# A mixture-of-experts kernel on one Trainium2 core: two pieces of row preparation change places on VectorE and on GpSimd

## What is computed

```python
def cond(hidden, ids):                      # adapter and layer norm, chosen per batch
    z = relu(hidden @ down_w[id] + down_b[id])
    y = hidden + z @ up_w[id] + up_b[id]
    return layernorm(y) * ln_g[id] + ln_b[id]
def ffn(h):                                 # h: 16 x 256 rows of 256
    p = softmax(h @ gate_w + gate_b)        # 8 experts, the two best, weights normalised
    out = h + mlp(h, shared weights)
    return out + sum over the two best e of weight_e * mlp(h, weights of expert e)
x = x + ffn(cond(x, itok))                  # mlp: 256 -> 1024, gelu, 1024 -> 256
```

## Time and profile before

| | |
|---|---|
| median of three runs | 622.54 us (621.13 to 623.94) |
| the profiled execution, its own time | 623.3 us |
| its span, from the first to the last instruction | 621.6 us |
| granted TensorE clock, mean | 0.993 |
| TensorE busy | 596.2 us, 96% |
| VectorE busy | 498.0 us, 80% |
| GpSimd busy | 404.6 us, 65% |
| ScalarE busy | 386.1 us, 62% |

### The profile page before, as it was taken

The page is one execution under the profiler, slowest core; times in us unless marked ns, Lnnn a source line. Parts: engine busy times, 40 slices in busy tenths (PEclk is TensorE's granted clock), DMA queues, the critical chain, the costliest instruction groups (busy, mean ns, idle before and its releaser), DMA issues.

```text
span 621.6 us, 16955 instructions
## 1 busy us (share of the span) xinstructions
PE 596.2 (96%) x5119; PEld 484.7 (78%) x5119; DVE 498.0 (80%) x1218; ACT 386.1 (62%) x666; POOL 404.6 (65%) x326
## 2 busy tenths in 40 slices
PE   7889999999999999999999999999999999999993
PEld 3556576677666678888878888888888999899882
DVE  3999878977867866998989898989897677888862
ACT  1776956776867747766676767676754455455450
POOL 3453868887646612559678686858697566666682
PEclk8999999999999999999999999999999999999998
DMA  8999679694675954676556766666634454243322
GB/s 282 291 221 244 175 177 290 146 271 110 155 120 182 289 135 149 145 124 143 122 128 105 147 129 140 129 139 128 94 50 71 62 67 61 54 67 64 45 25 28
DMA packets 119046, 85.52 MB, mean 138 GB/s; under 512 B 71346, under 2 KB 106418, under 8 KB 118962
## 3 DMA queue, kind: packets, MB, share of 16 engines
q1 hardware_dynamic: 100802, 60.64, 40.0%
q0 software_dynamic: 15600, 21.12, 20.2%
q10 hardware_dynamic: 2560, 2.69, 1.3%
HBM read 43.21 MB, written 24.42 MB: 109 GB/s over the span
## 4 chain that ended last, share of the span: by engine, by line
PE 77%; DMA 3%; DVE 2%; SPq 1%; issue 1%; another core or an unknown queue 0%; POOL 0%; ACT 0%; POOLq 0%; DVEq 0%
PE Y L1561 30%; PE H L1535 29%; PE Y L1453 9%; PE H L1438 7%; DMA xT<-wreg 2%; SPq L369 1%; DMA wreg<-wreg 1%; PE U L1372 1%; PE Z L1361 1%; DVE wreg L984 0%; DVE wreg L837 0%; POOLq L120 0%; DVE hh L1284 0%; DVE hl L1286 0%
## 5 line engine op out<-in xcount | busy, mean ns | idle before, releaser
L779 ACT ACTIVATE hf<-H,prme 128x256 f32<-128x256 f32 (+1 forms) x312 | 149.2, 544 | 93.4 <-issue 77.3
L1535 PE MATMUL H<-xT,wreg 128*128 128x256 f16 (+1 forms) x1872 | 194.3, 263 | 0.5 <-ACT hf L779 0.2
L1561 PE MATMUL Y<-wreg,hh 128*128 x1136 | 188.4, 273 | 1.1 <-DVE hl L1286 1.0
L1535 PEld LDWEIGHTS H<-xT,wreg 128*128 x1872 | 169.2, 98 | 18.9 <-issue 1.2
L1561 PE MATMUL Y<-wreg,hl 128*128 x568 | 154.8, 273 | 0.0
L1561 PEld LDWEIGHTS Y<-wreg,hh 128*128 128x128 f16 x1136 | 111.1, 98 | 15.8 <-issue 1.8
L1286 DVE SCALAR_TENSOR_TENSOR hl<-hf,prme,hh 128x512 f16<-128x512 f32 (+1 forms) x156 | 117.6, 754 | 5.5
L1284 DVE TENSOR_SCALAR hh<-hf,prme 128x512 f16<-128x512 f32 (+1 forms) x156 | 92.5, 593 | 29.2 <-ACT hf L779 26.8
L610 POOL DMA_INDIRECT out_y<-hl,xgm x38 | 69.6, 1832 | 60.4 <-DVE hl L1313 44.2
L599 POOL TENSOR_SCALAR b2w<-b2t,wsel 128x256 f32<-128x256 f32 x71 | 99.2, 1633 | 15.0 <-DVE wsel L1301 9.5
L557 POOL DMA_INDIRECT xs_rows<-wreg x64 | 73.3, 1145 | 29.3 <-issue 16.9
(11 more groups left out here) (208 smaller groups left out, 664.6 us busy)
## 6 DMA issues: line engine op xcount, KB each, us to landing
stage<-in_w SPq DMA_DIRECT2D x16, 1024.0 KB
b2t<-in_b SPq DMA_DIRECT2D x39, 128.0 KB
wreg<-in_wpack SPq DMA_DIRECT2D x16, 256.5 KB, 4.3
wreg<-in_xt SPq DMA_DIRECT2D x16, 256.0 KB
wreg<-in_vecs SPq DMA_DIRECT2D x16, 256.0 KB
wreg<-wreg POOLq DMA_DIRECT2D x16, 256.0 KB, 5.7
out_y<-wreg SPq DMA_DIRECT2D x16, 256.0 KB, 2.6
wreg<-in_x SPq DMA_DIRECT2D x14, 256.0 KB, 6.0
```

The lines of the kernel that those rows point to most:

```text
L779: act.activation(hf[:, c, half * w:(half + 1) * w], H[c][:, half * w:(half + 1) * w], ACT.Gelu_apprx_tanh, bias=pr[:, ch:ch + 1], scale=pr ...
L1535: m = pe.matmul(H[c][:, half * w:(half + 1) * w], we[:, bass.ds(e + h * 2048 + k * 1024 + col, P)], xp[:, a + k, 0:w], start=i == 0, stop= ...
L1561: m = pe.matmul(result(n, j), hx[:, n % 2, c * w + j * P:c * w + (j + 1) * P], we[:, bass.ds(e + 4096 + h * 2048 + c * D, D)], start=c == ...
```

## The change

```diff
@@ gpsimd_program, slot s
                 for p in at(s, 5):
                     rows(2 * p)
                     rows(2 * p + 1)
-                for p in at(s, 0):
+                for p in at(s, 1):
                     xb(2 * p)
-                for p in at(s, 1):
                     xb(2 * p + 1)
                 for p in at(s, 6):
                     residual(2 * p)
@@ vector_program, slot s
                 if s == 6:
                     choose(1)
+                for p in at(s, 6):
+                    if p > PT:
+                        low_rows(p)
                 for p in at(s, 2):
                     statistics(2 * p)
                 for p in at(s, 3):
...
                     order()
                 if s >= 6 and s % 2 == 0:
                     shared_rows((s - 6) // 2)
-                for p in at(s, 6):
-                    if p > PT:
-                        low_rows(p)
                 for p in at(s, 4):
                     roots(p)
```

## The result

The change makes the kernel slower: 629.51 us (median of 4 runs, 628.69 to 630.9) against 621.84 us (4 runs, 619.87 to 623.94), a ratio of 1.0111 with a 95% interval of 1.0077 to 1.0144. That is above the forecast of 623.0 and outside its range.

A forecast was written before the change was run, and what follows sets the result against it. The prediction took TensorE to bound the first stage, 96% busy with 6.1 us idle. Terms of +0.8 and -0.3 gave +0.5 us on 622.54, thus 623.0 us, range 619.9 to 626.3.

The forecast's parts named there:

- Part 3: Pair 3's transposes before `logits(3)`: `rows(6)`, `rows(7)` go ahead of `xb(8)`, but SyncE's queue holds; -0.3 us, from -1.48 to +1.
- Part 1: `xb(4)` behind `rows(2)`, `rows(3)` makes `statistics(4)` and `up(5)` 1.3 us late; +0.8 us stays from TensorE's stop at 49.97.
- Part 4: `low_rows(4)`, slot 13: pair 4's transposes start sooner, next `statistics` come two instructions of about 0.7 us later; zero.
- Part 6: Pair 6, slots 14 to 16: `xb(12)` ends later, pair 5's transposes start 2.6 us later without TensorE waiting; 0.
- Part 7: `low_rows(6)`, slot 20, 2.5 us sooner: the 0.75 us stop at 169.16 goes, given back at 183.92; 0, down to -1.55.
- The slower rival: SyncE held behind `xb(12)`: pair 5's transposes come too late for `logits(5)`, a 3.0 us stop; 626.0 us, chance 0.18.

The follow-up runs named there:

- kernels with copies: The kernel before and the changed kernel, whole or in part, with SyncE's transposing transfers replaced by copies; with plain copies 615.80 us before and 619.53 with the whole change.
- five bases: The kernel before with transposes replaced by plain copies, 256-byte pieces, 128-byte pieces, six copies or eight copies: 615.80, 613.70, 617.26, 617.57, 631.87 us.
- VectorE's half alone: Plain copies for transposes, only low rows moved ahead of the statistics, GpSimd as before: 621.58 us against 615.80 for the kernel before with plain copies.
- runs with plain copies: Transposing transfers replaced by plain copies of the same bytes in both kernels: before 615.80 us, whole change 619.53, GpSimd's half 616.79, VectorE's half 621.58.
- run of pieces: Not the kernel but pieces of it on made-up data; GpSimd additions beside VectorE operations took 2.2 us each, alone 1.2.

## Why the prediction was wrong

- **Part 3 failed, and decides.** Its term was -0.3 us, with +1 as the worst, for the transposes of pair 3. The stop before `logits(3)` went from 1.48 to 4.64 us, +3.2. The start of their issue was right to 0.2 us, and so was the reason that it could not move (SyncE's queue behind `xb(8)`). The sentence that the next residual transfers "start sooner and compete" had the mechanism; the bound of +1 had no working. It also took the 5.62 us of issue as fixed and looked for a change behind it only; 2.7 of the 3.15 us arose within the issue. The trace of before could have given an estimate: from 89.1 to 101.4 us the DMA engines passed 2.27 MB and were full, so each 0.185 MB moved ahead of the landing is 1 us. The 0.36 MB more that came by GpSimd's queue are 1.9 us.
- **The clock was left out of every term.** The sum priced a longer stop at its length. The stop of 4.64 us cost 1.57 us on top, in slower products behind it. Without it the two kernels would differ by some 3.8 us in the profiles (5.4 - 1.57).
- **Part 1** was right in place and size, and wrong in sum. `up(5)` waited 1.68 us where about 1.6 was forecast. But TensorE was 0.3 us earlier at slot 8, not 0.8 later. What was missed is `xb(4)`'s old place. VectorE and GpSimd before:

```profile
33.72 1.23 DVE L938 SCALAR_TENSOR_TENSOR wreg<-wreg 128x4 f32<-128x4 f32 x1
```

```profile
33.67 1.26 POOL L525 TENSOR_TENSOR wreg<-wreg 128x512 f32<-128x512 f32 x1
```

and VectorE after:

```profile
33.32 0.16 DVE L937 SCALAR_TENSOR_TENSOR wreg<-wreg 128x4 f32<-128x4 f32 x1
```

A tiny operation of the roots was held for 1.1 us behind `xb(4)`, and with it ScalarE and a stop of TensorE of 1.23 us at 38.37, which is now 0.17. I applied the lock-out to the place that `xb(4)` moved to and not to the one that it left. The gain and the cost cancel. The same shows in the kernels with copies: that stop is 1.1 to 1.2 us in four of the five bases (none in the fifth, nor with VectorE's half alone), and at most 0.2 in the kernels with `xb(4)` in its new place.
- **Part 4** was costed at zero for the two instructions that the statistics now wait for. In this trace that held at `up(9)`, as TensorE came later; in the runs with plain copies the same order cost 1.2 us there and 1.4 at `up(13)`. That the zero held here was luck: TensorE was late enough not to notice.
- **Part 6** put the trouble at SyncE: transposes of pair 5 2.6 us later (it had the adapter's load 3.2 us later and gave no reason why the transposes behind it lose only 2.6). They came 1 us later than TensorE's own shift (138.77 - 133.00 - 4.8), and `logits(5)` did not wait: that rival fell. What happened is the lock-out, now of four GpSimd operations in a row, on the low half that TensorE wanted:

```profile
131.04 2.50 POOL L535 TENSOR_TENSOR wreg<-wreg 128x512 f32<-128x512 f32 x2
133.50 2.48 POOL L525 TENSOR_TENSOR wreg<-wreg 128x512 f32<-128x512 f32 x2
```

```profile
131.76 5.31 DVE L1190 SCALAR_TENSOR_TENSOR hl<-hf,prm,hh 128x1024 f16<-128x1024 f32 x1 [1.86 <-issue]
```

5.31 us where it takes 1.28 alone. It did not get its turn between two of them, as in the run of pieces: GpSimd's four took 1.25 us each, as if alone, and VectorE's stood until the last was done. What decides between the two no run shows. TensorE waited 0.44 us for it, and slot 17 is 0.6 us later than slot 16's shift.
- **Part 7** was half right: the stop before `logits(6)` is gone, but it was not given back before `logits(7)`, which waited 0.74 us (0.80 before) and not 1.55. With it the lateness fell from 5.75 to 4.76 us.
- **The slower rival** had the sign and the wrong place; its 626.0 us is still 3.5 short. The first expert tile waits 1.17 us in the profile of after for something that the trace does not name, 0.21 before; that, and the 0.4 us between slots 12 and 16 (0.1 of it the last of the low clock, 2.87 us for 2.75 of the first products of slot 12), stay open.

## What to carry to other kernels

Where DMA engines are full beside a transfer that the bound engine waits for, a transfer that is moved earlier can be estimated in bytes over the rate of that stretch, and one that nobody waits for is better kept behind. Look at the landing and at the issue of the awaited transfer, and not only at the stop: a delay can be there and hidden. Where GpSimd and VectorE both work from SBUF, look for the lock-out at the place an operation leaves as well as at the one it takes. And price a long stop of the matmul engine twice, by its length and by the products behind it at half clock; in these runs, from 20 us on, that held for every stop of 2.58 us or more and for none up to 2.06.

## What was not expected of the hardware

- GpSimd's additions and VectorE's operations of two inputs can take turns one by one, 2.2 us each where 1.2 us alone, as in the run of pieces. They need not: in the changed kernel one VectorE operation stood for 5.31 us while four of GpSimd's ran in 1.25 us each.
- The clock fell to 0.50 behind a stop of 2.58 us and not behind 1.46, 1.62 or 2.06; it cost the eight passes of f32 products 3.10 us in place of 1.99.
- SyncE's issue of transfers is itself drawn out when GpSimd's transfers run: 5.62 to 8.59 us with transposes, 4.47 to 7.14 with copies in pieces of 128 bytes. With the transposes that is where 2.7 of the 3.15 us went.
- Plain copies of 128 KB landed in 2.1 us alone and in up to 4.5 beside two residual transfers.
